# One image's first scores ahead of the previous image's weighted sums, and layer-norm statistics one step later, in a one-core vision tower

## The reference

```
h = tok(x, ...)                                    # (16, 256, 192)
h = h + attn(layernorm(h))                         # 12 heads, causal softmax
h = h + ffn(layernorm(h))                          # 21 nodes, path of depth 11

scores = einsum("bqhd,bkhd->bhqk", q, k) / sqrt(16), causal mask
out    = softmax(scores) @ v  @ W_proj + b_proj
```

## Time and profile before

| | |
|---|---|
| median of 3 runs | 331.52 us (331.21 to 337.34) |
| the profiled execution's own time | 332.06 us |
| its span (first to last instruction) | 330.3 us |
| lies outside the span | 1.76 us |
| granted TensorE clock, mean over the span | 0.946 of full |
| TensorE busy | 267.7 us (81%) |
| VectorE busy | 224.9 us (68%) |
| ScalarE busy | 193.8 us (59%) |
| GpSimd busy | 186.3 us (56%) |

### The profile page before, as it was taken

The page is one execution under the profiler, slowest core; times in us unless marked ns, Lnnn a source line. Parts: engine busy times, 40 slices in busy tenths (PEclk is TensorE's granted clock), DMA queues, the critical chain, the costliest instruction groups (busy, mean ns, idle before and its releaser), DMA issues.

```text
span 330.3 us, 7883 instructions
## 1 busy us (share of the span) xinstructions
PE 267.7 (81%) x2638; PEld 207.2 (63%) x2638; DVE 224.9 (68%) x1126; ACT 193.8 (59%) x393; POOL 186.3 (56%) x322
## 2 busy tenths in 40 slices
PE   0469061187897989999999999999999999999873
PEld 0446051176776667767767767767767777776662
DVE  1054110055488779889888888898898897967872
ACT  2651022045445867867767767768767656858770
POOL 4727777400203567667676676576676575555662
PEclk9997658579999999999999999999999999999997
DMA  4712311001660824625625625624525423000038
GB/s 110 229 35 43 79 22 18 15 0 54 128 108 14 132 78 88 127 89 78 130 78 84 130 79 84 133 75 80 133 83 79 122 85 83 2 5 2 1 98 285
DMA packets 26720, 27.27 MB, mean 83 GB/s; under 512 B 6834, under 2 KB 26416, under 8 KB 26680
## 3 DMA queue, kind: packets, MB, share of 16 engines
q1 hardware_dynamic: 23176, 23.69, 31.7%
q0 software_dynamic: 1568, 2.36, 3.0%
q10 hardware_dynamic: 1936, 0.72, 0.8%
HBM read 4.34 MB, written 3.15 MB: 23 GB/s over the span
## 4 chain that ended last, share of the span: by engine, by line
PE 59%; DVE 10%; POOL 9%; ACT 6%; DMA 6%; issue 6%; SPq 3%; DVEq 0%; ACTq 0%; POOLq 0%
POOL G L342 9%; PE bank L1342 7%; PE bank L1364 7%; PE bank L1308 6%; PE bank L1257 4%; ACT PT L563 4%; PE bank L1279 3%; PE bank L1284 3%; PE bank L1367 3%; DMA G<-x,I 3%; SPq L295 2%; PE bank L1238 2%; PE bank L1304 2%; PE bank L1346 2%; DVE C L846 2%
## 5 line engine op out<-in xcount | busy, mean ns | idle before, releaser
L846 DVE CUSTOM_DVE_ANT_0 C<-bank,MASKV 128x256 bf16<-128x256 f32 (+1 forms) x384 | 112.8, 350 | 19.9 <-PE bank L1308 15.2
L563 ACT ACTIVATE PT<-bank 128x512 f32<-128x512 f32 x144 | 80.8, 598 | 35.0 <-PE bank L1342 30.5
L363 POOL TENSOR_SCALAR_AFFINE_SELECT PT<-PT 128x256 f32<-128x256 f32 x144 | 68.8, 485 | 52.6 <-ACT PT L563 48.6
L347 POOL TENSOR_TENSOR PART<-RES,PART 128x256 bf16<-128x256 f32 (+1 forms) x31 | 28.1, 906 | 25.7 <-ACT PART L557 25.7
L342 POOL DMA_INDIRECT G<-x,I x32 | 30.3, 948 | 15.3 <-issue 9.5
L802 DVE BATCH_NORM_STATS2 ST<-HT 128x6 f32<-128x192 f32 x32 | 9.5, 348 | 32.9 <-ACT HT L515 32.9
L846 DVE DVE_READ_ACCUMULATOR2_ANT MX<- 128x1 f32 x384 | 31.8, 83 | 0.1
L1342 PE MATMUL bank<-QS,KS 98*128 98x256 bf16 x144 | 27.9, 275 | 3.7 <-ACT PT L563 2.6
L1364 PE MATMUL bank<-PT,VA 128*32 128x256 f32 x384 | 30.5, 386 | 0.0
L1308 PE MATMUL bank<-KS,QS 96*128 96x256 bf16 x144 | 27.6, 273 | 1.4 <-DVE MX L846 1.0
L1159 PE MATMUL bank<-ID,G 128*48 128x128 f32 x32 | 6.7, 362 | 23.1 <-DMA G<-x,I 23.1
(11 more groups left out here) (165 smaller groups left out, 649.4 us busy)
## 6 DMA issues: line engine op xcount, KB each, us to landing
QS<-PART SPq DMA_DIRECT2D x72, 96.0 KB, 3.6
KS<-PART SPq DMA_DIRECT2D x72, 96.0 KB, 3.6
out<-HT SPq DMA_DIRECT2D x7, 384.0 KB, 3.6
KSL<-PART SPq DMA_DIRECT2D x24, 96.0 KB, 3.4
QSL<-PART SPq DMA_DIRECT2D x24, 96.0 KB, 3.6
G<-x,I POOLq DMA_INDIRECT x42, 2.5
out<-HT SPq DMA_DIRECT2D x2, 192.0 KB, 3.7
WFS<-wft ACTq DMA_DIRECT2D x2, 144.0 KB, 3.3
```

The lines of the kernel that those rows point to most:

```text
L347: pool.tensor_tensor(parts(b)[2][:, ROUNDS[w], :], RES[:, ROUNDS[w], :], parts(b)[1][:, ROUNDS[w], :], ALU.subtract).then_inc(p2_ok, 1)
L363: pool.affine_select(out=e, in_=e, compare_op=ALU.is_ge, fill=0.0, base=0, pattern=[[0, n], [1, P]], channel_multiplier=-1).then_inc(cut_o ...
L563: nc.scalar.activation(PT[:, v, :], BANK[T_BANK[(SU * par + v) % 2]][:, :], ACT.Exp, scale=SCALE).then_inc(exp_ok, 1)
L846: ins = nc.vector.tensor_tensor_reduce(JUNK[:, n:n + keys], bank[:, j * keys:(j + 1) * keys], MASKV[:, S - keys:S], 1.0, LOWEST, ALU.add, ...
```

## The change

TensorE: for the images 2 to 14 the wait for the stacked operands (`stack_in`, the same wait as before under a name) and the first unit of scores move from the head of the image's own step to the end of the step before, between `project_rest` and the first weighted group. In the middle of a step, `scores(b, par, 4)` moves one place ahead, past `scores_t(d, 1 - par, 3)`.

VectorE: the row maxima of that first unit follow, to between the two `heads_by_token` calls of the step before. The residual's statistics of image b - 2 leave the end of step b and come in step b + 1, behind `row_max(b, par, 5)`.

GpSimd: `low(f, 1)` goes ahead of `normalise(b - 1)`.

```
@@ pool, step(b)
                 biased(b)
+                if f.off < B:
+                    low(f, 1)
                 if not b.first:
                     normalise(b - 1)
-                if f.off < B:
-                    low(f, 1)
@@ vector, step(b, par)
-                row_max(b, par, 0)
+                if b.off == 1:
+                    row_max(b, par, 0)
...
                 row_max(b, par, 5)
+                if b.off >= 3:
+                    residual_statistics(b - 3)
                 if has_front:
                     rest(f, 0)
...
                 heads_by_token(d, False)
+                row_max(b + 1, 1 - par, 0)
                 heads_by_token(d, True)
                 over_sums(d)
-                if has_old:
-                    residual_statistics(b - 2)
@@ vector, closing_step(b, par)
-                row_max(b, par, 0)
+                if not b.late:
+                    row_max(b, par, 0)
...
                 row_max(b, par, 5)
+                if b.late:
+                    residual_statistics(b - 3)
@@ tensor
+            def stack_in(b, par):
+                for w in range(2):
+                    pe.wait_ge(stacked[w][par], 6 * 16 * (b.off // 2 + 1))
             def step(b, par):
-                for w in range(2):
-                    pe.wait_ge(stacked[w][par], 6 * 16 * (b.off // 2 + 1))
-                scores(b, par, 0)
+                if b.off == 1:
+                    stack_in(b, par)
+                    scores(b, par, 0)
...
                 scores_t(d, 1 - par, 2)
+                scores(b, par, 4)
                 scores_t(d, 1 - par, 3)
-                scores(b, par, 4)
...
                 scores(b, par, 8)
                 if b.off >= 2:
                     project_rest(b - 2)
+                stack_in(b + 1, 1 - par)
+                scores(b + 1, 1 - par, 0)
                 weighted(d, 1 - par, 0)
                 weighted(d, 1 - par, 1)
                 max_t(b)
```

## The result

The changed kernel takes 371.02 us (median of 4 runs, 368.37 to 377.5), the kernel before 331.37 us on the same chip. The ratio is 1.117, with a 95% interval of 1.108 to 1.127. The forecast was 365 us in a range of 355 to 378. The profiled execution of the changed kernel is its slowest one, at 377.5 us with a span of 375.8; 4.9 us of that are a late start of the program, by which single executions of one kernel differ here, and which the ratios leave out where the executions allow it.

The account below looks back on a forecast made before the run. Two coinciding limits: TensorE's work and the path from maxima through twelve issues to landing. First turn 3.1 us later, then twelve periods of 15.0 us, made +33.4 us on a 330.3 us span; 365 us as median, range 355 to 378.

Parts of the forecast that it names:

- The reading of the kernel before: Middle steps: two limits at once, TensorE's work and the path maxima, twelve issues, landing; no slack at the stack's wait.
- The closed loop: Moved wait puts the stack's landing on the way to the next maxima; period 15.0 us, before 12.47; chance 0.84.
- Leg one: From the maxima's issue on SP to the stack's last landing: 12.4 us, ends 12.0 and 13.3.
- the first turn: Step 1 waits for image 2's stack until 117.4 us; its maxima go out 3.1 us later than before.
- Rival 1: Stack transfers crowd each other less with a longer period; period 13.3 us, +13 us, 345 us; chance 0.06.
- The landing worked out from the Trainium skill: Stack's last transfer lands 2.2 us behind its issue, period 12.6 us, about +5 us in all; not used in the sum.
- Leg two: From the stack's landing through first scores and weighted groups to the next maxima's issue: 2.6 us, ends 2.5 and 2.8.
- The clock: TensorE's clock might fall behind idle spans at the stack's wait; single falls reach upward in the range, nothing in the sum.
- Rival 2: TensorE's clock falls to 1.2 GHz around the stack's wait; up to 25 us more, 390 us; chance 0.06 in full.
- The statistics: Behind unit 5 on VectorE they delay project_wide: 0.5 us a step if TensorE is the bound, nothing under the loop.
- The exponential's wait: scores(4) ahead of scores_t(3) fills TensorE's 0.24 us a step; alone up to 3.1 us, under the loop nothing.
- low(f, 1): Ahead of normalise on GpSimd, it can remove the 0.75 us hold between the stack's third and fourth issues.

Follow-up runs that it names:

- Experiment 9: Kernel before with low(f, 1) and scores(4) moved earlier, and the statistics one step later, ahead of row_max 5; 332.97 us, ratio 0.991.
- experiment 2: The whole change, but the stack's wait and first unit of scores stay at the head of their own step; 337.73 us, ratio 1.020.
- experiment 3: The whole change, but the stack's wait and first scores stand between max_t and the last weighted group; 341.28 us, ratio 1.029.
- experiment 7: The whole change, but the maxima's small DMA issues from ScalarE's queue and the next image's middle part is cast ahead of the maxima; 350.02 us, ratio 1.049.
- experiment 8: Kernel before with only low(f, 1) ahead of normalise and scores(4) ahead of scores_t(3); 330.05 us, ratio 0.991.
- experiment 1: Kernel before with only the stack's wait, the first unit of scores and its row maxima moved ahead; 388.69 us, ratio 1.176.
- experiment 4: The whole change with five dummy matmuls of 0.33 us each ahead of the stack's wait; 367.51 us, ratio 1.105.
- experiment 6: The whole change, but from image 4 on each stack transfer moves a quarter of its bytes; 351.11 us, ratio 1.053.

## Why the prediction was right

**The reading of the kernel before** held. The stack's landing stood at the point of its use, the second limit beside TensorE's work. Experiment 9 shows it from the other side: with TensorE's work at 11.9 us the landing binds.

**The closed loop** is shown, and not by the change alone. With the early first scores taken out 338 us are left (experiment 2), with the wait moved behind max_t 341 (experiment 3), and with the maxima taken out of the SP queue 350 (experiment 7), though the early wait is still in its place. What costs is not that the wait is early, but that the next maxima, and behind them the next stack, are queued behind it.

**Leg one** was 12.4 us by image 2, the row without a hold. It measures 12.0 to 13.0, 12.4 in the mean of the images 3 to 14, and 10.6 with a quarter of the bytes. Image 2's own was 13.0, and with the fall behind it the first turn was 4.9 us longer than before and not 3.1. Rival 1, in which a longer period lets the transfers crowd less, gave 10.7 and is refuted: with the period at 14.5 us and more the last landings still take 3.8 to 5.0 us, 4.4 in the mean. The crowd is the dozen itself. The landing worked out from the Trainium skill (DMA: Bandwidth & Descriptors, Anatomy of one DMA) does not hold here either. The page gives its fit for transfers that GpSimd issues, which the prediction did not say, and these are issued by SP. By its figures leg one would be 7.7 + 2.2 = 9.9 us, not the 10.0 of the prediction, whose "4.7 at the most" also overlooks the 4.9 us of the earlier trace rows. Neither enters the sum.

**Leg two** was taken as 2.6 us and is 2.44 where the clock is full. I counted 0.38 us for the first scores, but the first weighted group starts 0.32 us behind their start. And from that group to the maxima's issue it is 2.03 us (216.07 to 218.10), where it was 2.19. Over thirteen steps -2.1 us, which hides a part of the next term.

**The clock** is the term that was mis-sized. The prediction put it at "single falls", for which it reached upward in the range, and at nothing in the sum; that was too low. There were eight falls; leg two is 2.9 to 4.0 us in eight of the steps, together +8.0 us. The forecast has 300.0 - 105.05 = 195.0 us from the maxima of image 0 to those of image 13. With 8.0 - 2.1 for leg two and +0.8 for leg one that makes 201.7, and 201.7 are measured. In the medians it is 371 for 365. Rival 2 in full, 25 us more, is refuted: each fall costs 0.5 to 1.5 us of leg two and five of the thirteen turns have none.

**The statistics** cost 0.56 us a step at `project_wide` where TensorE is the bound (experiments 2 and 8) and nothing under the loop, where the change has the same 0.56 us wait and TensorE stands ahead of the first scores afterwards: as predicted, both. **The exponential's wait** goes. Outside the loop, together with low(f, 1), that is worth 0.3 us a step where the landing is in time, and 0.16 in the mean (experiment 8). **low(f, 1)** I held for an edit that takes away a hold of 0.75 us. That was right for the whole change, but I did not see that with the first scores moved the hold would grow to 1.3 us without it; experiment 1 missed its expectation by 16 us for this.

## What to carry to other kernels

Before a wait is moved ahead, ask what is queued behind it on its engine, and whether any of that starts the thing that the wait is for one turn later. If so, the turn becomes the sum of the two legs, if that is longer than the engine's own work. The same wait ahead of that work and behind it differs by 30 us here (experiment 3), and two limits that coincide in a profile, here TensorE and a queue of transfers, have to be named both before one of them is shortened (experiment 9).

## What the runs showed of the hardware

In the changed kernel TensorE's clock fell behind idle spans of 1.9 to 2.5 us, and of 4.2 us in the first turn; none of the other five turns, with 0.8 to 1.8 us, has a fall. The Trainium skill (TensorE: Matmul & The Clock Gate, Why this matters for your kernels) asks only for gaps under about 3 us, and seven of these eight falls do not agree with it. Matmuls that nobody reads kept the clock up (experiment 4). The idle span alone does not decide, though. In experiment 1 the clock stayed at full behind one of 2.60 us, as the 0.64 us of the weighted group show:

```profile
266.19 0.38 PE L1307 MATMUL bank<-KSL,QSL 96*128 96x128 bf16 x4 [2.60 <-issue]
266.50 0.64 PE L1367 MATMUL bank<-PT,VA 128*32 128x256 f32 x8
```

The clock's first rise does not come at the same time in each execution, and the start of the program goes with it. The timeline of TensorE at the same matmuls of the first layer, the changed kernel and then the kernel before:

```profile
15.87 3.68 PE L1187 MATMUL bank<-G2T,W2S 96*64 96x256 f32 x16 [0.67 <-ACT G2T L488]
```

```profile
15.96 1.95 PE L1182 MATMUL bank<-G2T,W2S 96*64 96x256 f32 x16 [0.67 <-ACT G2T L488]
```

The first execution has the full clock from 26.9 us on, the second from 15.0. The gathers that wait for TensorE went on at 27.32 us for 22.56, and image 0's maxima came at 109.92 for 105.05. All twelve profiled executions agree with this: with the rise at 15 to 16 us image 0's maxima come at 104.8 to 105.3 (five kernels), with the rise at 25.6 to 27.7 us at 108.8 to 110.1 (six), and with the rise at 19.3 us at 106.1 (one). What sets the time of the rise is open.

The small transfer of the maxima takes 3.1 us to land among three large ones from another queue (experiment 7). Ahead of the large ones on the same queue it takes 2.2, in the chain of experiment 6, where the large ones have a quarter of their bytes:

```profile
206.89 2.21 DMA QSL<-MT
```

The twelfth of a dozen 96 KB transfers lands 4.4 us behind its issue in the mean, the first 3.0. By the fit of the Trainium skill (DMA: Bandwidth & Descriptors, Anatomy of one DMA), which the page gives for transfers that GpSimd issues, it would be an estimated 2.2 us.
